# Local-attention scores computed with 64-row by 32-column tiles of the array, q kept without zero padding

## What is computed

```python
def attn_layer(x, Wqkv, qs, ksc, Wo):
    qkv = x @ Wqkv
    q, k, v = jnp.split(qkv, 3, -1)
    ...
    q = l2norm(q) * qs
    k = l2norm(k) * ksc
    q = q * cos * scale + rotate_half(q) * sin * scale
    k = k * cos * inv + rotate_half(k) * sin * inv
    out = local_attention(q, k, v)
    ...
    return out @ Wo

def local_attention(q, k, v):
    ...
    sim = jnp.einsum('bhwie,bhwje->bhwij', bq, bk2) * QK_SCALE
    sim = jnp.where(mask, -jnp.finfo(sim.dtype).max, sim)
    attn = jax.nn.softmax(sim, -1)
    out = jnp.einsum('bhwij,bhwje->bhwie', attn, bv2)
    ...

for i in range(DEPTH):
    x = attn_layer(shift_tokens(x), Wqkv[i], q_scale[i], k_scale[i], Wo[i]) + x
    x = ffn_layer(shift_tokens(x), ln_g[i], ln_b[i], W1[i], b1[i], W2[i], b2[i]) + x
```

## Time and profile before

| | |
|---|---|
| median of 3 runs | 1827.65 us (1826.91 to 1828.55) |
| the profiled execution, own time | 1827.32 us |
| its span, first to last instruction | 1825.5 us |
| TensorE busy | 1684.5 us (92%) |
| VectorE busy | 1678.9 us (92%) |
| GpSimd busy | 1528.1 us (84%) |
| ScalarE busy | 1451.8 us (80%) |
| mean granted TensorE clock | 0.981 of full speed |

### The profile page before, as it was taken

How to read it: one execution, slowest core, us unless ns; L and a number is a source line. 1 busy time by engine, 2 the same in 40 slices (tenths; PEclk the granted TensorE clock), 3 DMA queues, 4 the chain that set the end, 5 groups by cost and what they waited for, 6 DMA issues and landing times.

```text
span 1825.5 us, 58977 instructions
## 1 busy us (share of the span) xinstructions
PE 1684.5 (92%) x19888; PEld 1377.7 (75%) x19888; DVE 1678.9 (92%) x3652; ACT 1451.8 (80%) x2786; POOL 1528.1 (84%) x1079
## 2 busy tenths in 40 slices
PE   5789999899999899999999999989999989999995
PEld 4567778777777777787777778777787877787773
DVE  6699999999999999999999999999999999999982
ACT  2568888788888788888888888878888888888872
POOL 3498988898898889889888988988898889889970
PEclk9799999999999999999999999999999999999997
DMA  5010110011201101300110201011201100100110
GB/s 143 35 42 22 28 27 25 20 29 35 82 20 28 32 20 29 97 20 20 29 32 20 90 27 28 20 29 31 86 20 29 32 20 27 28 26 20 29 34 24
DMA packets 29942, 65.49 MB, mean 36 GB/s; under 512 B 4948, under 2 KB 16216, under 8 KB 29144
## 3 DMA queue, kind: packets, MB, share of 16 engines
q1 hardware_dynamic: 29912, 65.09, 12.4%
HBM read 19.99 MB, written 1.05 MB: 12 GB/s over the span
## 4 chain that ended last, share of the span: by engine, by line
PE 33%; ACT 28%; DVE 20%; issue 15%; ACTq 2%; DVEq 2%; SPq 0%; DMA 0%; POOL 0%; POOLq 0%
PE bank L1024 25%; ACT qz L584 4%; PE bank L1149 4%; ACT sq L562 4%; ACT pz L600 4%; ACT L592 3%; ACT L621 3%; DVE n L837 3%; DVE t L832 2%; PE bank L1180 2%; DVE s L871 2%; DVE es L866 2%; DVE rot L853 2%; ACT es L592 2%; DVE t L835 2%
## 5 line engine op out<-in xcount | busy, mean ns | idle before, releaser
L395 POOL TENSOR_TENSOR rot<-t 128x512 f32<-128x512 f32 x384 | 490.9, 1289 | 137.9 <-DVE t L835 137.9
L405 POOL TENSOR_TENSOR rnorm<-n2c,minus_half 128x16 f32<-128x16 f32 x192 | 576.3, 3001 | 15.3 <-DVE n2c L846 1.0
L1024 PE MATMUL bank<-w_hi,x_hi 128*128 128x512 f32 x576 | 284.3, 494 | 8.7 <-DVE t L835 5.6
L832 DVE TENSOR_TENSOR t<-bank,rtab 128x512 f32<-128x512 f32 x384 | 260.9, 679 | 29.7 <-ACT sq L562 19.6
L418 POOL TENSOR_TENSOR es<-es,r 128x512 f32<-128x512 f32 x192 | 206.2, 1074 | 92.8 <-DVE r L876 92.8
L837 DVE TENSOR_REDUCE n<-sq 128x8 f32<-128x512 f32 x384 | 259.6, 676 | 0.0
L600 ACT ACTIVATE pz<-bank 64x512 f32<-64x512 f32 x384 | 226.1, 589 | 41.7 <-PE bank L1180 35.9
L1149 PE MATMUL bank<-ident,rot 128*128 128x128 f32 x1536 | 238.1, 278 | 17.1 <-ACT qz L584 6.7
L1024 PEld LDWEIGHTS bank<-kt,qz 128*64 128x64 f32 x6144 | 203.8, 137 | 48.0 <-issue 48.0
L562 ACT ACTIVATE sq<-bank 128x512 f32<-128x512 f32 x384 | 224.5, 595 | 17.9 <-PE bank L1024 14.5
L584 ACT ACTIVATE qz<-bank 64x512 f32<-64x512 f32 x384 | 226.0, 589 | 10.2 <-PE bank L1149 5.5
(11 more groups left out here) (102 smaller groups left out, 3464.1 us busy)
## 6 DMA issues: line engine op xcount, KB each, us to landing
vb<-v SPq DMA_DIRECT2D x96, 384.0 KB, 3.4
w_new<-in_Wqkv SPq DMA_DIRECT2D x6, 1536.0 KB, 8.7
vb<-v SPq DMA_DIRECT2D x48, 128.0 KB, 2.3
w_o<-in_Wo SPq DMA_DIRECT2D x6, 512.0 KB
w<-in_W SPq DMA_DIRECT2D x6, 341.0 KB
b<-in_b SPq DMA_DIRECT2D x6, 341.0 KB
out<-acc SPq DMA_DIRECT2D x1, 1024.0 KB, 5.1
w<-in_W SPq DMA_DIRECT2D x12, 64.0 KB
```

The lines of the kernel that those rows point to most:

```text
L395: g.tensor_tensor(rot[:, i * CH:(i + 1) * CH], t1[:, b:b + CH], t2[:, b:b + CH], ALU.add)\
L405: g.tensor_tensor(rnorm[:, w], n2c[:, w], minus_half[:, :], ALU.pow).then_inc(s_rn, 1)
L832: d.tensor_tensor(heads(t1[:, b:b + CH]), src, table(n, kind, T), ALU.mult).then_inc(s_t1, 1)
L1024: return t.matmul(o, l, r, start=start, stop=stop, skip_group_check=True)
```

## The change

q is stored as it comes out of the transpose, tokens along the columns, in `qt` (8 pairs by 256 columns instead of 8 by 512); `qz` and its `memset` are gone. `take_qk` copies a chunk of q in one operation of 128 partitions, as it does one of k. In `scores` the 16 products of 128 rows by 64 columns become 32 products of 64 rows by 32 columns, one for each head and window, with the same 64 moving columns. The head of a pair (`hh`) picks the upper or the lower half of the rows, and pair and head together pick one of four column groups (`o` = 0, 32, 64, 96), so four products in a row have four different column groups, and the row halves alternate. `s_qte` counts 8 copies a step instead of 12, and the waits on it follow.

```diff
-        qz = sb("qz", PAIRS * 8 * 64)
+        qt = sb("qt", PAIRS * LEN)
...
-            g.memset(qz[:, :], 0.0)
             g.memset(kt[:, :], 0.0)
...
                 pr = slice(4 * (g % 2), 4 * (g % 2) + 4)
-                src = pT[:, :].rearrange("p (a w q) -> p a w q", a=4, w=4)
+                src = pT[:, :].rearrange("p (a t) -> p a t", a=4)
                 if g < 2:
-                    for h in range(2):
-                        r = slice(64 * h, 64 * h + 64)
-                        a.activation(qz5[r, pr, 4 * T:4 * T + 4, h, :], src[r], ACT.Copy).then_inc(s_qte, 1)
+                    dst = qt3[:, pr, T * P:(T + 1) * P]
                 else:
-                    a.activation(kt3[:, pr, WIN + T * P:WIN + (T + 1) * P],
-                                 pT[:, :].rearrange("p (a t) -> p a t", a=4), ACT.Copy).then_inc(s_qte, 1)
+                    dst = kt3[:, pr, WIN + T * P:WIN + (T + 1) * P]
+                a.activation(dst, src, ACT.Copy).then_inc(s_qte, 1)
...
-                    pe.wait_ge(s_qte, nth(12, n, 6 * T + (2 * g if g < 3 else 5)))
+                    pe.wait_ge(s_qte, nth(8, n, 4 * T + g))
...
-                for pair in range(PAIRS):
-                    odd = pair % 2
+                for half in range(PAIRS // 2):
                     for s in range(2):
                         w = 4 * T + al + 2 * s
-                        c = (pair // 2) * 128 + s * 64
-                        last = mm(pS[64 * odd:64 * odd + 64, c:c + 64],
-                                  qz[:, (pair * 8 + w) * 64:(pair * 8 + w) * 64 + 64],
-                                  kt3[:, pair, WIN * w:WIN * w + 64], start=False, stop=pair == PAIRS - 1)
+                        c = half * 128 + s * 64
+                        for odd in range(2):
+                            pair = 2 * half + odd
+                            for hh in range(2):
+                                r, o = 64 * hh, 64 * odd + 32 * hh
+                                last = mm(pS[o:o + WIN, c:c + 64],
+                                          qt3[r:r + DH, pair, WIN * w:WIN * w + WIN],
+                                          kt3[r:r + DH, pair, WIN * w:WIN * w + 64],
+                                          start=False, stop=half == PAIRS // 2 - 1)
```

More of the change, by code:

```diff
@@ L263, in over @@
             return a.unsqueeze(2).to_broadcast([P, k, w])
-        qz5 = qz[:, :].rearrange("p (a w h q) -> p a w h q", a=PAIRS, w=8, h=2)
+        qt3 = qt[:, :].rearrange("p (a t) -> p a t", a=PAIRS)
         kt3 = kt[:, :].rearrange("p (a t) -> p a t", a=PAIRS)
@@ L1096, in take_in @@
                 pe.wait_ge(s_xin, nth(1, n, 1))
-                pe.wait_ge(s_qte, nth(12, n - 1, 6))
+                pe.wait_ge(s_qte, nth(8, n - 1, 4))
                 for T in range(TILES):
@@ L1140, in turn_qk @@
                 if g == 0 and T == 0:
-                    pe.wait_ge(s_qte, nth(12, n - 1, 12))
+                    pe.wait_ge(s_qte, nth(8, n - 1, 8))
                 elif g == 0:
-                    pe.wait_ge(s_qte, nth(12, n, 6))
+                    pe.wait_ge(s_qte, nth(8, n, 4))
                     if live(n + 1):
@@ L1154, in scores @@
                 T, al = u // 2, 1 - u % 2
-                pe.wait_ge(s_qte, nth(12, n, 6 * T + 6))
+                pe.wait_ge(s_qte, nth(8, n, 4 * T + 4))
                 if u == 0:
```

## The result

The changed kernel takes **1760.19 us** (median of 4 runs, 1758.46 to 1761.86), the kernel before, run beside it on the same chip, 1828.1 us (1826.91 to 1828.87). The ratio is 0.963, with an interval of 0.961 to 0.965: 68 us faster. I had forecast 1812 us with a range from 1790 to 1850; the sign was right, the gain four times what I had worked out, and the time lies outside the range.

A forecast was written before the change was run, and what follows sets the result against it. VectorE was taken to bound the kernel, busy 33.48 of 35.0 us an iteration. 42 ordinary iterations at 0.35 (14.7 us) and five new-layer ones at 0.15 (0.75), off 1827.32, gave 1811.9, stated as 1812 us; range 1790 to 1850.

The forecast's parts named there:

- VectorE sets a floor of 33.5 us: Ordinary iteration of 35.0 us: VectorE busy in 33.48, so only its waits, 1.5 us, could be won.
- the wait before `values` at 820.55: TensorE's 0.23 us wait for take_o goes, but it then waits longer for middle; worth 0.
- the copy at 0.6 us a place: On ScalarE, one q copy replaces two at four places: 0.6 us each, 2.4 us of ScalarE's time an iteration.
- `down` as the place where it counts: TensorE's down waits for the last copy to ht, behind a q pair; it could start 0.40 us earlier.
- the stall before `sums`: VectorE's stall before sums(n, 1) falls from 0.49 to about 0.14 us; gain 0.35, bounds 0.2 to 0.49.
- the second q pair: The q copies at 807.73 end 0.6 plus 0.6 us earlier, at about 807.7, and hold nobody.
- d = 0: Extra time per score: 64 records on four column groups take 1.1 us as before; bounds 0.1 less to 1.1 more.
- a d above zero at `scores(n, 2)`: VectorE's maxima waits right behind this score, so any extra time in it would delay VectorE.
- four groups don't run as two: Rival: score records start no faster than one in 35 ns, 1.1 us more a score; 1960 us, chance 0.09.
- the row halves take turns: Rival: upper and lower row products can't write one bank together, d near 1.0 us; 1945 us, chance 0.07.
- More than that: Rival: VectorE's stalls before rotate and x_lo shrink too, ScalarE having 2.4 us less; 1790 us, chance 0.05.
- at most 0.15: Iterations of a new layer, where the stall before sums is 0.16 us: gain at most 0.15 us each.

The follow-up runs named there:

- e9: The changed kernel with only the clamp guard(nx, 0, 0) done as a reduction; 1747.91 us, ratio 0.957.
- e5: The changed kernel with one tiny VectorE memset of 128x1 ahead of guard(nx, 0, 1); 1812.01 us, ratio 0.991.
- e6: The changed kernel with two copies of 64 partitions again for only the first q chunk of each tile; 1818.23 us, ratio 0.996.
- e7: The changed kernel with two copies of 64 partitions again for only the second q chunk of each tile; 1758.78 us, ratio 0.964.
- e1: The changed kernel with all score products back in the old wide shape (scores not the right ones), single q copies kept; 1802.96 us, ratio 0.987.
- e2: The changed kernel with two copies of 64 partitions for every q chunk again, new score products kept; 1820.67 us, ratio 0.997.
- e3: The kernel before with the clamp of the norms done as a reduction at all four places; 1812.9 us, ratio 0.992.
- e4: The changed kernel with the clamp of the norms done as a reduction at all four places; 1793.22 us, ratio 0.982.
- e8: The changed kernel with only scores(n, 2) in the old wide product shape (those scores not the right ones); 1797.32 us, ratio 0.982.

## Why the prediction was wrong

*Wrong: "VectorE sets a floor of 33.5 us, and what can be won without taking work from it is what it waits for, 1.5 us."* This is the step that failed. The 33.48 us of the earlier trace rows hold 1.14 us in which VectorE stood blocked at this clamp, and more at others. The window after has 32.32 us, an ordinary iteration of e9 31.99, and in these too clamps and products are held: its own work is less than that. With that floor I had left room for 1.5 us at most and looked no further than VectorE's waits.

*Wrong, as its consequence:* the wait before `values` at 820.55, "Worth 0", since TensorE would then wait the longer for `middle`. That holds with the stall in VectorE (e5: 34.60 us). Without it the first-chunk copies cost 1.19 us together, a held clamp included (e6 against e7), twice what one place at 0.6 us can give. The 1.31 us of an iteration are thus 0.40 for the copies with the stall in place (the kernel before against e5) and 0.91 for the stall's end (e5 against the changed kernel).

*Right:* the copy at 0.6 us a place; `down` as the place where it counts; the stall before `sums` going from 0.49 to nearly nothing, 0.40 us an iteration; that the second q pair holds nobody (e7 costs nothing). With the stall in place e1 and e5 have iterations of 34.60 us, 0.40 less than before against my 0.35, and e5's time is my 1812 us. The time of the changed kernel itself I had no term for.

*Right in kind, small in size, large in effect:* the score. I took d = 0 with -0.1 as the lower bound; the runs show -0.10 us, at the bound. That bound came from a lighter weight load; whether that is the cause no run isolates. I had written that a d above zero at `scores(n, 2)` would make VectorE wait at `maxima`; I didn't ask what a d below zero would do there. It wins the race for the port, 1.14 us for 0.1.

*The rivals:* that four groups don't run as two, and that the row halves take turns, both fell: 64 records in 1.03 us are one in 16 ns. "More than that" had the right side but the wrong mechanism; the wait before `rotate` grew.

*New layers:* "at most 0.15" each, and they gave 3.3. Part of it goes with VectorE's split of the weights, 1.9 us shorter each time, again an instruction that meets GpSimd: 1079 ns before, here the changed kernel's group.

```profile
L806 DVE TENSOR_TENSOR w_lo<-w_new,w_hi 128x512 fp32r<-128x512 f32 x36 | 27.8, 814 | 0.0
```

That is 9.5 us over the whole run. e5, with the clamp late again, has 1083 ns and layer changes of 40 to 41.7 us. The rest of the 3.3 us I didn't take apart.

## What to carry to other kernels

Before busy time is taken as a floor, look at how long each kind of small instruction takes at each place: the same 128x16 operation at 0.17 and at 1.31 us means that it was blocked, and the floor is lower by the difference. Where two things hold an iteration at nearly the same length, removing either alone shows little (4 and 22 us here, 68 together), so an edit is to be tried with the other one taken away as well. Before such a run is read, look whether the stall that it removes has come up at another instruction: in e2, e3 and e4 it had. And a stall that comes from who is first at a port can be moved by 0.1 us anywhere ahead of it, to a better or a worse place: after each edit compare the mean of every instruction that can meet GpSimd, not only of the one that was mended.

## What the runs showed of the hardware

- Four tiles of 64 rows by 32 columns run at once, though both row halves write one bank (different partitions of it): 64 float32 records of 64 moving columns in 1.03 us, 16 ns each, where 32 records on two tiles took 1.13. In the trace the records start in fours, 6 or 7 ns apart within a four, and most fours follow each other by 56 ns. The Trainium skill says in "TensorE: Matmul & The Clock Gate", section "Wait — 56ns, not 53.3ns?", that starts never come closer than about 25 ns, and in "TensorEngine Tiling (Array Packing)", section "Gotcha 1: PSUM Pressure", that different row tiles can't access one bank at the same time. Neither held here, and the measurement decides. The first didn't hold in the kernel before either, where about half of the records start 3 to 14 ns behind the one ahead of them.
- A VectorE instruction that is blocked by GpSimd is recorded as busy, not as idle: the clamp of 0.17 us with 1.31, the product of 0.68 with 1.76, the weights' split with a mean of 1.08 instead of 0.81. No view of waits shows it. It goes the other way as well: GpSimd's addition of 1.28 us took 1.88 where the clamp and the product came first. The reduction of 128x32 to 128x16 took 0.17 to 0.19 us wherever it stood.
- Who wins at `guard(nx, 0, 1)` can be the same in every iteration (VectorE in 44 of 44 after, GpSimd in 44 of 44 in e5) or in most (GpSimd in 32 of 44 before), and it turns with the shape of one score ahead of it (0.1 us; e8, where GpSimd wins 33 of 44) or with one operation on one column in VectorE's queue.
